# The maxima of a blocked attention: high and low part made ahead of one transpose, which goes through a bank of the energies

## The reference

```python
h = _sln(hidden, w, ln_g, ln_b, Wg, bg, Wb, bb)
qkv = (h @ Wqkv.T + bqkv).reshape(B, N, num_heads, hd, 3)
q = jnp.moveaxis(qkv[..., 0], 2, 1)
k = jnp.moveaxis(qkv[..., 1], 2, 1)
v = jnp.moveaxis(qkv[..., 2], 2, 1)
energy = jnp.einsum('bhqd,bhkd->bhqk', q, k)
att = jax.nn.softmax(energy, axis=-1) / D ** 0.5
out = jnp.einsum('bhqk,bhkd->bhqd', att, v)
```

## Time and profile before

| | |
|---|---|
| median of three runs | 874.18 us (872.0 to 874.53) |
| span of the profiled execution | 872.2 us |
| TensorE busy | 829.4 us, 95% |
| VectorE busy | 680.4 us, 78% |
| ScalarE busy | 459.2 us, 53% |
| 512 energies, L1555 | 184.1 us, 450 ns each |
| 512 exponentials, L1122 | 267.0 us, 603 ns each |
| 256 maximum reductions, L2097 | 302.1 us, 1221 ns each |
| 16 turns on TensorE, L1544 | 278 ns each |
| 16 casts and 16 subtractions, L2107 and L2108 | 269 and 278 ns each |

### The profile page before, as it was taken

The page is one execution under the profiler, slowest core; times in us unless marked ns, Lnnn a source line. Parts: engine busy times, 40 slices in busy tenths (PEclk is TensorE's granted clock), DMA queues, the critical chain, the costliest instruction groups (busy, mean ns, idle before and its releaser), DMA issues.

```text
span 872.2 us, 13436 instructions
## 1 busy us (share of the span) xinstructions
PE 829.4 (95%) x5042; PEld 526.0 (60%) x5042; DVE 680.4 (78%) x1160; ACT 459.2 (53%) x840; POOL 227.2 (26%) x377
## 2 busy tenths in 40 slices
PE   5999999999999999999989989999999999999993
PEld 3667888988998998887835433343334333433342
DVE  7998667778558578647458979999999999999377
ACT  4746232143432443333232168878887888888760
POOL 4433512203003003112012620333333333333411
PEclk9999999999999999999989989999999999999998
DMA  8613132110000000000696600505050515000102
GB/s 310 260 50 98 49 99 99 49 53 1 1 1 1 2 1 1 1 1 1 183 212 152 255 1 3 94 21 93 21 94 21 93 22 99 23 25 21 27 25 73
DMA packets 29379, 57.40 MB, mean 66 GB/s; under 512 B 7228, under 2 KB 15152, under 8 KB 29314
## 3 DMA queue, kind: packets, MB, share of 16 engines
q1 hardware_dynamic: 22596, 44.40, 19.5%
q0 software_dynamic: 6720, 12.15, 4.8%
HBM read 39.26 MB, written 14.91 MB: 62 GB/s over the span
## 4 chain that ended last, share of the span: by engine, by line
PE 81%; DVE 11%; ACT 4%; issue 2%; DMA 1%; POOL 1%; SPq 0%; DVEq 0%; ACTq 0%
PE PA L1555 15%; PE PA L1566 14%; PE PD L1342 10%; PE PA L1320 8%; PE PD L1526 6%; PE PA L1431 5%; PE PD L1400 4%; PE PA L1268 3%; PE PA L1387 3%; PE PA L1261 2%; DVE NMX L2097 1%; PE PD L1624 1%; PE PA L1501 1%; PE PA L1421 1%; ACT R L1122 1%
## 5 line engine op out<-in xcount | busy, mean ns | idle before, releaser
L2097 DVE TENSOR_REDUCE NMX<-PD 128x2 f32<-128x1024 f32 x256 | 302.1, 1221 | 23.6 <-PE PD L1526 19.1
L1122 ACT ACTIVATE R<-PA 128x512 f32<-128x512 f32 x512 | 267.0, 603 | 70.2 <-PE PA L1555 68.5
L1555 PE MATMUL PA<-STKR 50*128 50x512 f32 x512 | 184.1, 450 | 3.8 <-ACT R L1122 2.7
L1555 PEld LDWEIGHTS PA<-STKR 50*128 50x128 f32 x512 | 82.3, 186 | 151.4 <-ACT R L1122 140.8
L1526 PE MATMUL PD<-STKR 48*128 48x512 f32 x512 | 148.4, 452 | 2.3 <-DVE NMX L2097 2.3
L1058 ACT ACTIVATE R<-PA,VEC 128x512 f32<-128x512 f32 x64 | 43.8, 687 | 104.1 <-PE PA L1320 91.6
L1342 PE MATMUL PD<-WHR,HSR 128*128 128x256 f32 x512 | 95.4, 286 | 0.5 <-DVE HSR L1942 0.5
L1342 PEld LDWEIGHTS PD<-WHR,HSR 128*128 128x128 f32 x512 | 82.1, 191 | 6.1 <-issue 2.0
L1320 PE MATMUL PA<-XSR,WHR 128*128 128x512 f32 x256 | 81.2, 398 | 3.8 <-issue 2.0
L1526 PEld LDWEIGHTS PD<-STKR 48*128 48x128 f32 x512 | 61.0, 186 | 28.1 <-DVE NMX L2097 13.8
L1941 DVE CAST HSR<-R 128x512 fp32r<-128x512 f32 x64 | 28.4, 444 | 57.8 <-ACT R L1058 57.8
(11 more groups left out here) (301 smaller groups left out, 1216.9 us busy)
## 6 DMA issues: line engine op xcount, KB each, us to landing
STKR<-qk_terms SPq DMA_DIRECT2D x32, 384.0 KB, 8.6
R<-in_l_w SPq DMA_DIRECT2D x8, 1024.0 KB, 5.1
W<-in_w SPq DMA_DIRECT2D x4, 1024.0 KB, 10.2
qk_terms<-PARTS SPq DMA_DIRECT2D x8, 512.0 KB, 3.7
qk_terms<-PARTS POOLq DMA_DIRECT2D x8, 512.0 KB, 3.4
S<-row_reciprocals POOLq DMA_DIRECT2D x56, 64.0 KB, 2.1
X<-in_x SPq DMA_DIRECT2D x4, 512.0 KB, 9.7
qk_terms<-PARTS SPq DMA_DIRECT2D x8, 256.0 KB, 4.6
```

Source lines behind the costliest of these rows:

```text
L1122: act.activation(PB[:, n % 2, j, :], PA[:, e % NEB, :], ACT.Exp).then_inc(s_exp3, 1)
L1555: pe.matmul(PA[:, e % NEB, :], KS[rows, slot(gg), jj, kt * P:(kt + 1) * P], QS[rows, slot(gg), jj, c * HALF:(c + 1) * HALF], start=True, s ...
L2097: ve.tensor_reduce(out, PD[:, o:o + NROW, :], axis=AX_X, op=ALU.max, negate=True).then_inc(s_mred, 1)
```

## The change

The two parts are made before the transpose, on 128 partitions x 16 in the order queries x maxima, and one transpose turns both:

- `max_high` on ScalarE rounds `NMC` into the first 16 columns of a new tile `NMP` (in step 8m-5, ahead of the fourth exponential); it waits for the join.
- `max_low` on VectorE subtracts and fills the other 16 columns (in step 8m-4, between the two reductions).
- TensorE transposes `NMP`, 128 x 32, into the bank of energy (n, 0), once exponential (n, 0) has read it. This stands in step 8m-3, between energy(n, 2) and `times_v(n-1)`. Energy (n, 3), which uses that bank, waits for its copy.
- `max_turned` on ScalarE copies the bank, 32 x 128, into `NMT` (ahead of the fourth exponential of step 8m-3). SP's four DMAs wait for that.
- VectorE's cast and subtraction on the turned maxima are gone, and so is the turn's place in the alternation of the `PD` pairs.
- For unit 0 the same is done by `th`, `tl` and `tm` in the table, in a numbered bank of `PA`.

```diff
 def turn_step(m):
-    return NT * m + (UNIT - LEAD) // 2 + 1
+    return NT * m + (UNIT - LEAD) // 2 + 2
...
-SOLO = turn_step(NUNIT - 1) + 1
+SOLO = turn_step(NUNIT - 1)
...
+    if EARLY == UNIT + 1:
+        SCHED.append(("th", 0))
+    if EARLY >= UNIT + 3 and ("tm", 0) not in SCHED:
         SCHED.append(("tm", 0))
...
             for m in range(NUNIT):
-                sp.wait_ge(s_mred, MJ[("turn", m)] + 1)
+                if m:
+                    sp.wait_ge(s_nmt, m)
+                else:
+                    evacuated(sp, 0, "tm")
...
+            def max_high(m):
+                act.wait_ge(s_nmc, m + 1)
+                act.activation(NMP[:, 0:UNIT], NMC[:, :], ACT.Copy).then_inc(s_nmh, 1)
...
+            def max_turned(n):
+                m = TURN[n]
+                act.wait_ge(s_nmf, m)
+                nmrow_in(act, m - 1)
+                act.activation(NMT[:, :], PA[0:NPART * UNIT, (n * GH) % NEB, 0:P], ACT.Copy).then_inc(s_nmt, 1)
...
                     if j == 3 and kt == 0 and m >= 1:
                         copy_heads_out(m - 1)
+                    if j == 3 and n in TURN:
+                        max_turned(n)
+                    if j == 3 and n + 2 in TURN:
+                        max_high(TURN[n + 2])
...
-                pe.wait_ge(s_nmc, m + 1)
-                o = pair_bank("turn", m)
-                pe.transpose(PD[0:UNIT, o, 0:P], NMC[:, :], ident[:, :]).then_inc(s_mfull, 1)
+            def turn_max(m, o):
+                pe.wait_ge(s_nml, m + 1)
+                return pe.transpose(o[0:NPART * UNIT, 0:P], NMP[:, :].bitcast(F32), ident[:, :])
...
+            def turn_in_step(n):
+                e = n * GH
+                pe.wait_ge(s_exp3, e + 1)
+                turn_max(TURN[n], PA[:, e % NEB, :]).then_inc(s_nmf, 1)
...
+                if j == 3 and step in TURN:
+                    pe.wait_ge(s_nmt, TURN[step])
...
                 energy(n, 2)
+                if n in TURN:
+                    turn_in_step(n)
                 if n >= 1:
                     times_v(n - 1)
-                if n in TURN:
-                    turn_max(TURN[n])
                 energy(n, 3)
...
-            def turned_max(m):
-                o = PD[0:UNIT, pair_bank("turn", m), 0:P]
-                if m >= 1:
-                    nmrow_in(ve, m - 1)
-                link(ve.tensor_copy(NMT[:, 0, :], o))
-                ve.tensor_tensor(NMT[:, 1, :], o, NMT[:, 0, :], ALU.subtract).then_inc(s_mred, 1)
+            def max_low(m):
+                ve.wait_ge(s_nmh, m + 1)
+                ve.tensor_tensor(NMP[:, UNIT:], NMC[:, :], NMP[:, 0:UNIT].bitcast(F32), ALU.subtract).then_inc(s_nml, 1)
```

More of the change, by code:

```diff
@@ L188, in act_jobs @@
         return [(0, "ad", b)]
-    if stage in ("gg", "ba", "gr", "gc", "gk", "lr"):
+    if stage in ("gg", "ba", "gr", "gc", "gk", "lr", "tm"):
         return [(b, stage)]
@@ L246, in max_jobs @@
     if stage == "step":
-        turn = [("turn", TURN[n])] if n in TURN else []
-        return turn + [("max", LEAD + 2 * n + i) for i in range(2) if LEAD + 2 * n + i < NMAX]
-    return [("turn", n)] if stage == "tm" else []
+        return [("max", LEAD + 2 * n + i) for i in range(2) if LEAD + 2 * n + i < NMAX]
+    return []
 def number(jobs_of):
@@ L530, in build @@
         s_nmc = sem("negmax_joined")
+        s_nmh = sem("negmax_high_ready")
+        s_nml = sem("negmax_low_ready")
+        s_nmf = sem("negmax_turned_full")
+        s_nmt = sem("negmax_turned_copied")
         s_nmrow = [sem(f"negmax_rows{m % 4}") for m in range(4)]
@@ L1102, in g, with first_max_turned @@
                                    ACT.Gelu).then_inc(s_aev, 1)
+            def max_high(m):
+                act.wait_ge(s_nmc, m + 1)
+                act.activation(NMP[:, 0:UNIT], NMC[:, :], ACT.Copy).then_inc(s_nmh, 1)
+            def first_max_turned(m):
+                act.activation(NMT[:, :], bank(m, "tm")[0:NPART * UNIT, 0:P], ACT.Copy).then_inc(s_aev, 1)
+            def max_turned(n):
[3 more added lines that the diff above has]
+                act.activation(NMT[:, :], PA[0:NPART * UNIT, (n * GH) % NEB, 0:P], ACT.Copy).then_inc(s_nmt, 1)
             def copy_heads_out(m):
@@ L1131, in _ @@
                  "qk": qk, "att": att("att"), "az": att("az"), "x2": copied("x2", lambda b: X2T[b]), "a1": rank_rows("a1", 0), "a2": rank_rows("a2", 1),
-                 "g": g, "qk3": qk3, "step": step})
+                 "g": g, "qk3": qk3, "th": max_high, "tm": first_max_turned, "step": step})
             assert all(by_dve for by_dve, _ in AE[seen[0]:])
@@ L1598, in step @@
                 if n == SOLO - 1:
-                    hold["d"] = lambda: pe.wait_ge(s_mred, len(MJ))
+                    hold["d"] = lambda: pe.wait_ge(s_mred, NMAX)
                 if n == NSTEP - 1:
@@ L1650, in _ @@
                  "a2": down("a2", lambda b: GT, 1, gelu_ready), "f2": f2,
-                 "n3": turn("n3", lambda b: XN[:, b], "f2"), "qk3": qk3, "v3": v3, "mx": maxpass, "tm": turn_max,
+                 "n3": turn("n3", lambda b: XN[:, b], "f2"), "qk3": qk3, "v3": v3, "mx": maxpass, "tm": first_turn,
                  "step": step, "hd": heads_turned, "hx": heads_back, "p3k": p3_ahead, "p3a": p3_first, "p3": p3})
@@ L2117, in step @@
                 m, kt = divmod(n, NT)
-                for tag, x in max_jobs("step", n):
-                    (turned_max if tag == "turn" else reduce_max)(x)
+                jobs = [x for _, x in max_jobs("step", n)]
+                for x in jobs[:1]:
+                    reduce_max(x)
+                if n + 1 in TURN:
+                    max_low(TURN[n + 1])
+                for x in jobs[1:]:
+                    reduce_max(x)
                 if kt == 5 and 1 <= m < NUNIT - 1:
```

17 lines of the change are left out of this document (10 added, 7 removed).

## The result

| | before | after |
|---|---|---|
| median of the runs, us | 873.9 (4 runs, 872.0 to 874.5) | 886.69 (4 runs, 885.0 to 888.1) |
| ratio to before | | 1.015, interval 1.0129 to 1.0171 |
| span of the profiled execution | 872.2 | 886.1 |
| steps 8m-5, 8m-4, 8m-3, us | 2.61, 2.81, 2.61 | 2.96, 2.59, 3.42 |
| the same three steps in the last unit | 2.60, 2.81, 2.60 | 2.96, 2.59, 2.88 |

What follows compares the result with a forecast made beforehand. The prediction took a loop of latencies between TensorE and ScalarE as the bound. Its terms, 5.6 + 0.9 + 0.1 = 6.6 us, raised the median from 874.18 to 880.8 us, range 877.5 to 886.5.

Steps and rivals of the forecast that it cites:

- The loop of latencies: In the last attention, a step's 2.62 us is a chain of waits between TensorE and ScalarE, not a full TensorE.
- Term A: ScalarE's rounding in step 8m-5 waits for the join, delaying the fourth exponential 0.37 us per unit, 15 times: 5.6 us.
- Term B: The turn (transpose) in its new place, step 8m-3, delays the fourth energy by 0.06 us, 15 times: 0.9 us.
- What the change removes: VectorE drops a cast and subtraction per unit and gains one 128x16 subtraction, covered by 0.24 us of waiting: worth nothing.
- Term C: At the start, the first turn also waits for a 0.18 us low part: 0.1 us, between -0.4 and 0.2.
- The rows on SP's queue: Four DMAs after the turn, now a step later, still land with 1.7 us to spare before an energy reads them: nothing.
- Rival 1: TensorE is full, so ScalarE's idle time swallows the rounding and the copy: no change, 874.2 us; chance 0.07.
- rival 2: VectorE is the bound, and its two small operations go for one: 5.6 us faster, 868.6; chance 0.03.
- Rival 3: The turn between two kinds of tiles costs TensorE a second drain: 3.4 us more, 884.2; chance 0.14.

## Why the prediction was right and where it failed

- **The loop of latencies** as the bound: right. Steps without a turn keep 2.60 us, the step with the copy 2.70, and halving VectorE's work moves nothing. All that was reckoned by its links came out to 0.02 us.
- **Term A**, 15 x 0.37 = 5.6: 15 x 0.35 = 5.3 measured. X3 starts 0.15 us behind the join's end (584.30 to 584.45), for which I had 0.17. Taking that wait away alone gave 5.7 us in the medians (886.69 to 881.02), though only 2.0 by the ratios, with the run at 891.8 among its four; the steps show it (2.96 to 2.60).
- **Term B**, 15 x 0.06 = 0.9: this is the term that was mis-sized. It measured 0.59 in 14 units and 0.06 in the last, 8.3 us. Inside it all that I worked out is right: the turn 0.49 behind E2, `times_v` 0.20 behind the turn, the copy done in time, the turn step 2.88 us where nothing else waits. What is missing is a wait.
- **The step that failed** is in "What the change removes": the low part on VectorE, "its cover is the 2.60 - 2.36 = 0.24 us in which VectorE, after the two reductions of a step, waits for TensorE anyway", and "Nothing". Term B has the same gap: the turn "can start at 1.14" there, by the end of X0 alone. The quoted sentence asks whether VectorE has room for 0.18 us. It never asks when the result is there, and who waits for it. The change's own text says that it stands between the two reductions of step 8m-4, the order listing that the turn waits for `negmax_low_ready`, and the earlier trace rows has the reductions: two from 580.90 to 583.26. Those stand behind the join, but the step ahead of it, without a join, has the same distance (X3 at 578.06, the reduction at 578.30). Put together in the manner of term A, a first reduction of 1.18 us that begins 0.23 us behind X3's start (580.67 and 580.90) ends 1.41 behind it; the low part 0.18 more, a start 0.05 later: the turn at 1.64 instead of 1.14, 0.50 us, 14 times, 7.0 us, and a forecast of 887.8. The trace of before was enough for that. For the rounding I checked the readiness of the input and the queue behind; for the low part only the room.
- **Term C**, 0.1: 0.08. **The rows on SP's queue** had their slack: no energy waits for them.
- **Rival 1** (no change) and **rival 2** (VectorE is the bound, faster) fell, the second also by two experiments: VectorE, busy for 46.70 of 50 us, could lose 20 us of its work in that stretch for a ratio of 1.0003. The Trainium skill (Perfetto Trace Analysis, Identifying the Most-Contended Engine) would have the engine of highest occupancy optimized first; in this stage the runs don't bear that out for VectorE.
- **Rival 3** (a second drain): it decides, as I wrote, by the gap from turn to `times_v`, and that is 0.20 us with 32 columns between two kinds of tiles. It falls. Its time, 884.2, is nearer to the result than mine, and would have looked like a proof had only the time been known: the loss came in the very step that it names.
- **The range** ended at 886.5, since it took the bounds of the terms that I had; a term valued at nothing had a bound of 3 us only in VectorE's own time.

## What to carry to other kernels

- In a loop of latencies the question about a small operation that is moved is not whether its engine has room, but two others: is its input ready when its turn in the queue comes, and is its result there when the consumer could start. Write both times down for each such operation. The place in the queue cost 0.54 us for an instruction of 0.17, while its input lay ready for 3.9 us.
- How busy an engine is doesn't tell what its work costs: halving VectorE's reductions changed nothing in the kernel before (46.70 of 50 us busy), and took back four fifths of the loss in the changed one (43.57 of 50).
- A wait that the profile puts down to one engine, when another semaphore of the same wait fell later, is found by comparing the end times of all that is waited for with the start.

## What the runs showed of the hardware that was not expected

TensorE's granted clock falls to the lower of its two levels (0.50, 1.2 GHz) at two places of this program, where stages meet, in some kernels or executions and not in others, and this moves as much time as most of the edits.

- In the first steps, behind a stretch in which TensorE waits for reductions (busy 3.68 of 5 us in the row above). Before and after in one window:

```profile
505.00:511.00 6.00, 4.23 (x19) 1.76 (x16) 3.86 (x4) 4.84 (x8) 2.01 (x3) 0.51 0.00 0
```

```profile
505.00:511.00 6.00, 4.96 (x20) 2.56 (x22) 2.80 (x3) 4.00 (x9) 0.96 (x2) 0.56 0.00 0
```

 Before has one step of 4.07 us (the first); after has two, and a third of 3.15. That is the 1.65 us of the account. It is no effect of the change: the second execution of the changed kernel has 42.93 us from X3 of step 0 to X3 of step 15, the 41.05 of before and two units' 0.94, and no such loss; and the kernel before with the table early has two steps of 4.07 us as well.
- In steps 117 to 119, behind the three steps without maxpasses: 6.1 us in the kernel with the early low part (15.28 us for three steps; the mean clock of all its runs is 0.979 to 0.981, of after's profiled one 0.986), none in after. Matmuls that nobody reads removed it there (0.57 to 1.00 in the stretch, 0.986 to 0.988 in all six runs). A shorter step is thus not always a shorter kernel: here the clock took 6.1 of the 7.6 us that the steps had given. The kernel before isn't clear of it by its times: 3 of its 21 runs in the second set lie at 876.7 to 878.9 us with a mean clock of 0.980 to 0.982, the others at 871.0 to 874.3 with 0.985 to 0.987. None of the three was profiled, so where their clock fell stays open.
- A small activation behind another costs ScalarE 0.12 to 0.13 us of its row and not its 0.21 (the rounding at 584.33, X3 at 584.45). The 32 x 128 copy ahead of X3 costs nothing for another reason: in the last unit it is done at 832.23, before E3, for which X3 waits, even starts (832.39).
